# Batch 0's context quantised by column blocks with attention in between, later context turned by DMA, flips of context and weight scales moved to later tiles

## The chip, the core and the metric

One core of one Trainium2 chip. The engines of the core run their own programs, which meet at semaphores: PE (TensorE, matmuls), DVE (VectorE), ACT (ScalarE), POOL (GpSimd) and SP (SyncE, which here issues all loads, stores and DMA transposes). PEld is PE's weight load, which the profile lists apart from the matmul. The metric is the device time of one execution in microseconds (us).

## The reference

x is 4 batches of 512 tokens of width 512, ctx has the same shape. Two residual steps:

```python
x = x + _L0_xattn_ref(_layernorm(x), ctx_2048)        # xq @ wq^T, both quantised
x = x + _L0_ffn_ref(_layernorm(x), ...)

xq = quant_dequant_act_1x128(x)            # fp8 with one scale per token and 128 columns
wq = quant_dequant_weight_128x128(weight)  # fp8 with one scale per 128x128 block
return jnp.einsum('emk,enk->emn', xq, wq)

probs = jax.nn.softmax(xt @ w_router); topk_p, topk_idx = jax.lax.top_k(probs, 4)
basis = jax.nn.silu(xt @ w_gate) * (xt @ w_up)         # 8 bases of 256 columns
mixed = jnp.einsum('tek,tki->tei', mix[topk_idx], basis)
out = sum_e coeff_e * (mixed_e @ w_down)
shared = silu(xt @ shared_w_gate) * (xt @ shared_w_up) @ shared_w_down
return out + shared
```

The first step takes the batch's whole context (512 rows) as the weight: every tile of a batch needs all of it, quantised and turned so that columns lie on partitions.

## The kernel before

The 2048 tokens go in 16 tiles of 128; tiles 4b to 4b+3 belong to batch b. For each tile t the kernel does: layernorm of x; quantising it by blocks of 128 columns (DVE `quantise_x`: maxima, scale, mask; POOL `round_x`: an add and a subtract with a mask that rounds to the fp8 grid); turning x (PE `turn_x` in tiles 0 to 2, a DMA transpose from SP later); four attention matmuls `attend(t, kc)`, one for each block of 128 columns, into two PSUM tiles that take turns (even, odd); DVE `attention(t, kc)` scales each and adds it to x; layernorm to z (DVE `stats2`, ACT `norm2`, DVE z_lo); turning z as two fp16 halves (PE in tiles 0 and 1, SP's `turn_z` later); router logits (`route`), top four (DVE `largest`, `pick`), coefficients; five pairs of gate and up matmuls, p = -1 (the shared expert) and 0 to 3, whose results ACT (`silus`), DVE (`combine`) and POOL join; and the down projection `down(s)` of the tile before.

The matmuls of the gate, up and down weights run as three fp16 products (hi·hi, hi·lo, lo·hi). Tile 0 has no halves yet: `pair32` uses the fp32 weights as they were loaded, while ACT (`split_w`) and DVE (`lo_w`) make the halves chunk by chunk in tiles 0 and 1. There are twelve weight chunks in six groups (0,3), (3,5), (5,7), (7,9), (9,11), (11,12); the last chunk, DOWN, holds the down weights. A group's scale takes: ACT `sum_w` of each chunk, PE `flip_w` (the sums onto a few lanes), DVE `lane_w` (their maximum, a power of two, a small diagonal), PE `spread_w` (back to all 128 partitions), DVE `scales_w`. The context's scales go the same way, with DVE `max_ctx` in place of the sums: `flip_ctx(b)`, `lane_ctx`, `spread_ctx(b)`, `scales_ctx`.

The context of a batch is four chunks of 128 rows, c = 4b to 4b+3. Each is scaled (`scale_ctx`), masked on DVE (`mask_ctx`, two passes), rounded (`round_ctx`, two passes) into one of two `ctx_q` buffers, turned on PE (`turn_ctx`, four 128x128 transposes into the PSUM tile `turned[0]`) and copied by ACT (`keep_ctx`) to `ctx_qT`. For batch 0, DVE scales chunks 0 and 1 and rounds 2 and 3, ACT scales 2 and 3, POOL rounds 0 and 1; all four chunks are turned before the first attention matmul. For batch 1, ACT scales in tile 1. For batches 2 and 3, POOL scales. The turns of a later batch lie in two tiles of the batch before it; `ctx_turns(t)` gives them as `early` and `late`: all four of batch 1's in tile 2, batch 2's in tiles 5 and 6, batch 3's in tiles 9 and 10.

All of this is one function, `build`, which writes each engine's program out by hand, in order. PE's begins at the profile's line 1124; flips, spreads, turns and attention matmuls that belong to other work are put between two column steps of a pair by a dictionary: `pair32(0, {4: lambda: spread_w(2)})` puts the spread ahead of step 4 of the eight (four of gate, four of up). Of a tile t from 1 on, pair -1 and pair 0 carry the attention of tile t + 1, pair 2 its route; down(t - 1) stands behind pair 0 (down(0) at the end of tile 1). DVE's order begins at line 1556, ACT's at 765; SP's issues of a tile stand in the loop that begins at line 491. On every engine what is queued behind a waiting instruction waits too. PE's transposes share the two PSUM tiles `turned`, and the lists `uses0` and `uses1` say in which order, so that each user waits for the one before it.

The lines of before that the rows name:

| line | what |
|---|---|
| L899, L905 | PE `flip_ctx`, `spread_ctx` |
| L912, L920 | PE `flip_w`, `spread_w` |
| L929, L937, L969 | PE `turn_ctx`, `turn_x`, `turn_z32` (tile 0's z in fp32) |
| L954, L985, L1032 | PE `attend`, `pair32`, `pair` |
| L1014 | PE `route` |
| L1207, L1215 | DVE `max_ctx`, the lane's maximum in `lane_ctx` |
| L1233, L1239, L1242 | DVE `scale_ctx`, the two passes of `mask` |
| L1272, L1288 | DVE `stats`, first pass of `quantise_x` |
| L1317 | DVE `attention` |
| L1508, L1523, L1532 | DVE `lane_w`, `scales_w`, `lo_w` (gate_up, router and down halves) |
| L560, L567 | POOL `round_x`, add and subtract |
| L646, L655, L706 | ACT `sum_w`, `scale_ctx`, `norm2` of tile 0 |
| L460 | SP `turn_z`, low half |

Of the kernel before, what the change touches and what calls it, by code (L numbers as in the profile page):

```python
# [29 lines left out]
P = 128  # L30
# [43 lines left out]
def build(nc, x, ctx, w_router, w_gate, w_up, w_down, amplitudes, expert_scale,  # L74
# [35 lines left out]
    with ExitStack() as stack:  # L110
# [135 lines left out]
        ctx_scaled_dve, ctx_scaled_act, ctx_scaled_pool = sem("ctx_scaled_dve"), sem("ctx_scaled_act"), sem("ctx_scaled_pool")  # L246
# [3 lines left out]
        xT_in = sem("xT_in")  # L250
        zT_in = [sem("zT_hi_in"), sem("zT_lo_in")]
# [48 lines left out]
        def uses0():  # L300
# [3 lines left out]
            for t in range(1, TILES):  # L304
                front = t + 1 < TILES
                early, late = ctx_turns(t)
                if t % NB == 2 and t > 2:
                    early, late = late[:1], late[1:]
                out += [("coef", t)] + [("ctx", c) for c in early]
                out += [("ctx", c) for c in late] + [("weight", t + 1)] * front  # L310
            return out

        def uses1():
# [75 lines left out]
        def _(sp):  # L389
            def load_ctx(b, k):  # L390
                c = b * NB + k
                if b > 0:
                    wait_ctx_rounded(sp, c - NB)
# [7 lines left out]
            def load_chunk(n):  # L401
# [65 lines left out]

            def store(s):
# [22 lines left out]
            for t in range(TILES):  # L491
# [27 lines left out]
        def _(pool):  # L519
# [10 lines left out]
            def scale_ctx(c):  # L530
# [1184 lines left out]
```

## Time and profile before

| | |
|---|---|
| time, median of 3 runs (lowest to highest) | 588.35 us (586.7 to 589.03) |
| the profiled execution's own time | 587.09 us |
| its span in the trace, granted TensorE clock | 585.3 us, 0.994 |
| PE busy | 539.1 us, 92% of the span |
| DVE, ACT, POOL busy | 393.6 (67%), 242.8 (41%), 200.5 (34%) |
| chain of work that ended last | PE 73%, DVE 9%, issue 3%, ACT 2%, POOL 1% |
| DMA | 36.98 MB on queue q1, 23.4% of 16 engines |

The trace is of one execution, so its durations add up to its own 587.09, of which 585.3 is the span of the trace; the median stands 1.26 above it. PE is busy for 92% of the span as a mean, but the stages differ: a start without expert matmuls, tile 0 in fp32, tile 1 in which halves are still being made, and fourteen tiles after that. The rows that follow give the busy time for each stage. In brackets behind an instruction of a timeline stands the idle time of its engine just before it, with what released it. A clock of 1.00 in a row is TensorE's full clock.

### The profile page before, as it was taken

To read this page: it belongs to the slowest core of one execution; us is meant where nothing else is said; L and a number is where in the kernel's file an instruction comes from. 1 tells how busy PE (TensorE), PEld (TensorE's weight loads), DVE (VectorE), ACT (ScalarE), POOL (GpSimd) and SP (SyncE) were. 2 spreads that over 40 slices of the span, in tenths; PEclk is the share of its full clock that TensorE was granted. 3 is DMA by queue.
4 is the path that set the end of the run, shared out by engine and by line. 5 is a ranking of instruction groups with operands and counts; after the bars stand their busy time and mean duration, and the time that the engine had idled before them with its cause. 6 is when DMAs were issued, how large, how long until landed. Compare 5 with 4: busy or idle time off the path is not lost.

```text
span 585.3 us, 7951 instructions
## 1 busy us (share of the span) xinstructions
PE 539.1 (92%) x2624; PEld 257.8 (44%) x2624; DVE 393.6 (67%) x1123; ACT 242.8 (41%) x357; POOL 200.5 (34%) x236
## 2 busy tenths in 40 slices
PE   0359979789999999999999999999999999999997
PEld 0124434334544444454444444444444444444445
DVE  6977888788766577858574777768474757563322
ACT  4687885552524232342434242343433333423310
POOL 2431052443713126544413135634414131411110
PEclk9999999989999999999999999999999999999999
DMA  8724521011212413102113212111132111111110
GB/s 282 274 90 143 179 92 28 18 29 45 55 37 47 116 36 91 37 27 55 36 29 98 65 38 54 37 47 45 28 63 29 41 50 29 45 28 36 29 36 19
DMA packets 61657, 37.49 MB, mean 64 GB/s; under 512 B 48688, under 2 KB 49456, under 8 KB 61616
## 3 DMA queue, kind: packets, MB, share of 16 engines
q1 hardware_dynamic: 61616, 36.98, 23.4%
q8 instruction: 21, 0.34, 0.2%
q14 instruction: 20, 0.16, 0.1%
HBM read 21.24 MB, written 4.19 MB: 43 GB/s over the span
## 4 chain that ended last, share of the span: by engine, by line
PE 73%; DVE 9%; issue 3%; ACT 2%; POOL 1%; DVEq 0%
PE up L1032 29%; PE gate L1032 29%; PE even L1062 9%; PE odd L1014 2%; DVE x L1317 1%; DVE part L1409 1%; PE even L954 1%; PE odd L954 1%; DVE before L1356 1%; DVE gate_up L1532 1%; DVE down_lo L1532 1%; DVE ctx_m L1239 0%; PE up L1089 0%; PE gate L1089 0%; PE odd L1074 0%
## 5 line engine op out<-in xcount | busy, mean ns | idle before, releaser
L1032 PE MATMUL gate<-gate_up,zT_hi 128*128 128x512 f16 x592 | 177.0, 381 | 0.1
L1032 PE MATMUL up<-gate_up,zT_hi 128*128 128x512 f16 x592 | 177.1, 381 | 0.0
L731 ACT ACTIVATE silu<-gate,w_back 128x512 f32<-128x512 f32 x74 | 50.8, 687 | 170.4 <-PE gate L1032 169.5
L1032 PE MATMUL gate<-gate_up,zT_lo 128*128 128x512 f16 x296 | 112.9, 381 | 0.0
L1032 PE MATMUL up<-gate_up,zT_lo 128*128 128x512 f16 x296 | 112.7, 381 | 0.0
L1409 DVE SCALAR_TENSOR_TENSOR part<-up,coef,silu 128x256 f32<-128x256 f32 x126 | 55.0, 478 | 49.0 <-PE up L1032 40.6
L1032 PEld LDWEIGHTS gate<-gate_up,zT_hi 128*128 128x128 f16 x592 | 57.9, 100 | 65.2 <-issue 1.4
L589 POOL TENSOR_TENSOR hid<-hid,part 128x256 f32<-128x256 f32 x47 | 34.6, 736 | 148.2 <-DVE part L1409 148.2
L1032 PEld LDWEIGHTS up<-gate_up,zT_hi 128*128 128x128 f16 x592 | 57.0, 98 | 62.3 <-issue 1.1
L573 POOL TENSOR_TENSOR gain<-var,minus_half 128x1 f32<-128x1 f32 x16 | 11.3, 703 | 131.8 <-DVE neg_mean L1331 131.8
L1032 PEld LDWEIGHTS up<-gate_up,zT_lo 128*128 128x128 f16 x296 | 29.1, 98 | 35.3 <-issue 0.8
L1032 PEld LDWEIGHTS gate<-gate_up,zT_lo 128*128 128x128 f16 x296 | 29.0, 98 | 35.3 <-issue 0.6
L1317 DVE SCALAR_TENSOR_TENSOR x<-odd,both_scale,x 128x128 f32<-128x128 f32 x128 | 35.9, 342 | 11.1 <-PE odd L954 11.1
L695 ACT ACTIVATE y<-x,shift,gain 128x512 f32<-128x512 f32 x16 | 13.0, 812 | 57.1 <-POOL shift L575 57.1
L591 POOL TENSOR_TENSOR hid<-hid,part 128x256 f32<-128x256 f32 x47 | 34.3, 729 | 3.7
L560 POOL TENSOR_TENSOR x_v<-x_v,x_m 128x512 f32<-128x512 f32 x16 | 24.4, 1522 | 18.0 <-DVE x_m L1242 18.0
L1345 DVE TENSOR_SCALAR logit<-odd,w_back 128x128 f32<-128x128 f32 x15 | 5.2, 349 | 34.7 <-PE odd L1014 34.7
L544 POOL TENSOR_TENSOR ctx_in<-ctx_in,ctx_m 128x512 f32<-128x512 f32 x14 | 18.7, 1337 | 18.9 <-DVE ctx_m L1242 18.9
L1062 PE MATMUL even<-down_hi,hT_hi 128*128 128x512 f16 x90 | 22.4, 386 | 1.5 <-DVE x L1317 1.5
L586 POOL TENSOR_TENSOR hid<-part 128x256 f32<-128x256 f32 x16 | 12.0, 751 | 31.9 <-DVE part L1409 31.9
L1317 DVE SCALAR_TENSOR_TENSOR x<-even,both_scale,x_in 128x128 f32<-128x128 f32 x64 | 18.0, 344 | 7.1 <-PE even L954 7.1
L668 ACT COPY ctx_qT<-turn 128x512 bf16<-128x512 bf16 x16 | 9.3, 584 | 30.2 <-PE turn L929 30.2
(211 smaller groups left out, 840.5 us busy)
## 6 DMA issues: line engine op xcount, KB each, us to landing
ctx_in<-in_ctx SPq DMA_DIRECT2D x16, 256.0 KB, 4.0
x_in<-in_x SPq DMA_DIRECT2D x16, 256.0 KB, 2.9
out<-y_out SPq DMA_DIRECT2D x15, 256.0 KB, 2.2
stage<-in_L_ffn_w_gate SPq DMA_DIRECT2D x2, 1024.0 KB, 8.0
stage<-in_L_ffn_w_up SPq DMA_DIRECT2D x2, 1024.0 KB, 5.1
stage<-in_L_ffn_shared_w_gate SPq DMA_DIRECT2D x1, 1024.0 KB, 8.7
stage<-in_L_ffn_shared_w_up SPq DMA_DIRECT2D x1, 1024.0 KB, 9.8
ctx_qT<-in_L_ffn_w_up SPq DMA_DIRECT2D x1, 1024.0 KB, 12.9
```

The costliest lines, as they stand in the source:

```text
L544: ch.did(nc.gpsimd.tensor_tensor(ctx_in[:, k], ctx_in[:, k], ctx_m[:, k % 2], ALU.add))
L560: ch.did(nc.gpsimd.tensor_tensor(x_v[:], x_v[:], x_m[:], ALU.add))
L586: nc.gpsimd.tensor_tensor(mixed, one, two, ALU.add).then_inc(mix_acc, 1)
L589: nc.gpsimd.tensor_tensor(mixed, mixed, one, ALU.add).then_inc(mix_acc, 1)
L591: nc.gpsimd.tensor_tensor(mixed, mixed, two, ALU.add).then_inc(mix_acc, 1)
L695: nc.scalar.activation(y2[:], x2[:, t % 3, :], ACT.Identity, bias=shift2[:], scale=gain2[:]).then_inc(y2_done, 1)
L731: nc.scalar.activation(silu[:, k % 2, :], gate_ps[k % 2][:], ACT.Silu, scale=w_back[:, n:n + 1] if t else 1.0 / LN_GAIN).then_inc(silu_don ...
L954: nc.tensor.matmul(ps[:], x_qT[:, kc, :], ctx_qT[:, t // NB, kc, :], start=True, stop=True).then_inc(att_full, 1)
L1032: mm = nc.tensor.matmul(ps[:], zT[a][:, t % 2, kc, :], wgu[:, n - 1 + i, w, kc, :], start=(m == 0), stop=(m == 3 * KC - 1))
L1062: mm = nc.tensor.matmul(even_ps[:], hT[a][:, hc, :], wd[w][:, hc, :], start=(n == 0), stop=(n == 3 * HC - 1))
L1317: ch.did(nc.vector.scalar_tensor_tensor(x2[:, t % 3, cols], ps[:, cols], both_scale[:, nb, kc:kc + 1], prev, ALU.mult, ALU.add))
L1409: ins = nc.vector.scalar_tensor_tensor(part[:, p % 2, cols], up_ps[k % 2][:, cols], coef[:, t % 2, KPC * p + i:KPC * p + i + 1], silu[:, k ...
```

## The change

What is computed, and the loads and stores, stay. Six things move.

1. **Batch 0's context by columns.** The `c` of batch 0's `scale_ctx`, `mask_ctx`, `round_ctx` and `turn_ctx` now means a block of 128 columns of all four row chunks (`ctx_cols`), which is what one `attend(0, kc)` needs. Blocks 0 and 2 are scaled on ACT, 1 and 3 on POOL; DVE masks and rounds all four and does attention of block kc - 2 after block kc. PE turns block by block with `attend` in between. The views are strided: 4 pieces of 128 columns a partition.
2. **Tile 0's x.** DVE takes its maxima (`measure_x`) ahead of the context's lane, and rounds it itself (`round_x`), where POOL did.
3. **Later contexts.** The twelve `turn_ctx` on PE and their `keep_ctx` on ACT go; SP issues twelve `dma_start_transpose`, early ones ahead of `turn_z(t + 1)`, late ones behind it. All of them are rounded on POOL as before.
4. **Scales of batch 1's context.** The maxima are the last thing on DVE in tile 1 (before: in the middle of it), flip and spread and lane come in tile 2, and ACT scales all four chunks in a row in tile 2 (before: two and two in tile 1).
5. **Scales of the weight groups 4 and 5.** Flips and spreads move from the last pair of tile 0 to the first two pairs of tile 1, `lane_w` and `scales_w` from tile 0 to the head of tile 1, `sum_w(DOWN)` on ACT into tile 1. In tile 0 the flips and spreads of groups 0 to 3 move by some steps.
6. **Small moves.** `norm2(0)` and `keep_z32` on ACT ahead of the first weight splits, `turn_x(2)` to the head of tile 1 from two steps later, `lo_w(DOWN)` on DVE ahead of `largest(2)`, `mask_ctx` of early chunks behind `combine(t, 0)`.

```diff
@@ uses1(): order of the second turning tile
-            out = lane("ctx", 0) + lane("w", 0) + [("x", 0)] + lane("w", 1) + [("x", 1)]
-            out += lane("w", 2) + lane("w", 3) + [("z", 1)] + lane("w", 4) + lane("w", 5)
+            out = lane("ctx", 0) + [("x", 0)] + lane("w", 0) + [("flip_w", 1), ("x", 1), ("spread_w", 1)]
+            out += lane("w", 2) + lane("w", 3) + [("z", 1)] 
...
+        def ctx_cols(kc):
+            return ctx_in[:, :, kc * P:(kc + 1) * P]
...
@@ SP
+            def turn_ctx(c):
+                b, k = c // NB, c % NB
+                if c == NB:
+                    wait_ready(sp, DOWN)
+                sp.wait_ge(ctx_round_pool, CTX_ROUNDS * (c - NB + 1))
+                sp.dma_start_transpose(ctx_qT[:, b, :, k * P:(k + 1) * P], ctx_q[:, c % 2, :]).then_inc(ctxT_in[c % 2], 16)
...
+                for c in early:
+                    turn_ctx(c)
                 if 2 <= t + 1 < TILES:
                     turn_z(t + 1)
+                for c in late:
+                    turn_ctx(c)
                 if 3 <= t + 2 < TILES:
                     turn_x(t + 2)
...
@@ POOL scale_ctx
-                nc.gpsimd.tensor_tensor(c4(ctx_in[:, k]), c4(ctx_in[:, k]),
-                                        ctx_mul[:, k].unsqueeze(2).to_broadcast([P, KC, P]), ALU.mult
+                rows, by = (ctx_cols(c), ctx_mul[:, :, c]) if c < NB else (by_block(ctx_in[:, k]), ctx_mul[:, k])
+                nc.gpsimd.tensor_tensor(rows, rows, by.unsqueeze(2).to_broadcast([P, KC, P]), ALU.mult
...
@@ ACT
+                if t == 2:
+                    for c in range(NB, 2 * NB):
+                        scale_ctx(c)
...
@@ PE attend(t, kc)
-                    pe.wait_ge(kept0, turn_of(HI, "ctx", t // NB * NB + NB - 1) + 1)
+                    if t >= NB:
+                        for i in range(2):
+                            pe.wait_ge(ctxT_in[i], 8 * NB * (t // NB))
...
@@ PE tile 0
-            pair32(3, {0: lambda: route(1), 1: lambda: flip_w(4), 4: lambda: spread_w(4), 5: lambda: flip_w(5)})
-            spread_w(5)
...
+            pair32(-1, {4: lambda: flip_w(1), 6: lambda: turn_x(1)})
+            pair32(0, {2: lambda: [spread_w(1), attend(1, 0)], 4: lambda: attend(1, 1), 7: lambda: flip_w(2),
+                       6: lambda: attend(1, 2)})
+            pair32(1, {0: lambda: [turn_weight(0), attend(1, 3)], 2: lambda: spread_w(2), 3: lambda: coefs(0),
+                       7: lambda: flip_w(3)})
+            pair32(2, {2: lambda: spread_w(3), 6: lambda: [turn_z(1, HI), turn_z(1, LO)]})
+            pair32(3, {0: lambda: route(1)})
...
@@ PE tile t
+                    shared[0] = lambda: turn_x(2)
+                    shared[5] = lambda: flip_w(4)
+                if t == 2:
+                    shared[3] = lambda: flip_ctx(1)
...
+                    zero[0] = lambda: [spread_w(4), coefs(1)]
+                    zero[4] = lambda: flip_w(5)
+                    zero[7] = lambda: spread_w(5)
+                if t == 2:
+                    zero[1] = lambda: spread_ctx(1)
...
@@ DVE start
+            x_chain = measure_x(0)
             scales_ctx(lane_ctx(0), 0)
-            scale_ctx(0)
-            scale_ctx(1)
-            mask_ctx(0)
-            mask_ctx(1)
-            quantise_x(0)
-            lane_chain = lane_w(0)
...
+            shrink_x(x_chain, 0)
+            round_x(0)
+            for kc in range(KC):
+                mask_ctx(kc)
+                round_ctx(kc)
+                if kc >= 2:
+                    attention(0, kc - 2)
+            attention(0, 2)
             stats(1)
+            attention(0, 3)
+            stats2(0)
```

How the built programs stand, one instruction or a run of like ones a row (line, operation, out<-in, shape, count). First PE from the flip of batch 0's context scales to the first expert matmul, which is L985 before and L983 after; `turn` is the PSUM tile of transposes, `even` and `odd` those of attention. Before:

```order
L899 MATMUL turn<-ident,ctx_max 16x128
L905 MATMUL turn<-lane_diag,ones 128x16
L929 MATMUL turn<-identb,ctx_q 128x128 x4
L912 MATMUL turn<-ident,w_max 3x128
L920 MATMUL turn<-lane_diag,ones 128x3
L929 MATMUL turn<-identb,ctx_q 128x128 x8
L937 MATMUL turn<-identb,x_q 128x128 x4
L929 MATMUL turn<-identb,ctx_q 128x128 x4
L954 MATMUL even<-ctx_qT,x_qT 128x512
L954 MATMUL odd<-ctx_qT,x_qT 128x512
```

After:

```order
L931 MATMUL turn<-identb,x_q 128x128 x4
L923 MATMUL turn<-identb,ctx_q 128x128 x8
L952 MATMUL even<-ctx_qT,x_qT 128x512
L923 MATMUL turn<-identb,ctx_q 128x128 x4
L952 MATMUL odd<-ctx_qT,x_qT 128x512
L906 MATMUL turn<-ident,w_max 3x128
L923 MATMUL turn<-identb,ctx_q 128x128 x4
L952 MATMUL even<-ctx_qT,x_qT 128x512
L952 MATMUL odd<-ctx_qT,x_qT 128x512
L959 MATMUL turn<-ident,y 128x128 x4
L914 MATMUL turn<-lane_diag,ones 128x3
```

x is turned ahead of all context, the attention matmuls stand between the turns, and the first flip and spread of weight scales (L912, L920 before, L906, L914 after) go behind the second attention matmul and behind z's turn.

Then ACT in tile 2, from the shared silu of tile 2 (`hs_hi` is the half that `down(1)` needs, `hid_abs` the shared expert's sums, `y`, `z_hi` the norm of tile 3). Before:

```order
L744 ACTIVATE hs_hi<-hid,hid_scale 128x768
L731 ACTIVATE silu<-gate,w_back 128x512
L738 ACTIVATE hid_abs,shared_sum<-hid 128x512
L695 ACTIVATE y<-x,shift,gain 128x512
L701 ACTIVATE z_hi<-x,shift,gain 128x512
L677 ACTIVATE y<-x_in,neg_mean 128x512
```

After:

```order
L761 ACTIVATE hs_hi<-hid,hid_scale 128x768
L748 ACTIVATE silu<-gate,w_back 128x512
L675 ACTIVATE ctx_in<-ctx_in,ctx_mul 128x128 x16
L755 ACTIVATE hid_abs,shared_sum<-hid 128x512
L712 ACTIVATE y<-x,shift,gain 128x512
L718 ACTIVATE z_hi<-x,shift,gain 128x512
```

The scaling of all four chunks of batch 1 now stands between the silu of pair 0 and the sums and norm behind it; before, it was done in tile 1.

Last SP in tile 2, from the stores of tiles 0 and 1 to the turn of tile 4's x. Before:

```order
L470 DMA out<-y_out 128x512 x2
L458 DMA_TRANSPOSE zT_hi<-z_hi 128x4x128
L460 DMA_TRANSPOSE zT_lo<-z_lo 128x4x128
L466 DMA_TRANSPOSE x_qT<-x_q 128x4x128
L399 DMA x_in<-in_x 128x512
```

After:

```order
L483 DMA out<-y_out 128x512 x2
L479 DMA_TRANSPOSE ctx_qT<-ctx_q 128x4x128 x2
L462 DMA_TRANSPOSE zT_hi<-z_hi 128x4x128
L464 DMA_TRANSPOSE zT_lo<-z_lo 128x4x128
L479 DMA_TRANSPOSE ctx_qT<-ctx_q 128x4x128 x2
L470 DMA_TRANSPOSE x_qT<-x_q 128x4x128
```

Two turns of context now stand ahead of the turn of tile 3's z, and two between it and the turn of x.

## Rows read from the trace of the kernel before

**Rows 1.** Stretches of the span: length, busy us per engine (instructions), PE clock, DMA.

```profile
40.20:86.07 45.87, 41.70 (x127) 18.50 (x127) 36.46 (x98) 38.99 (x42) 13.00 (x12) 1.00 0.40 132
86.07:127.83 41.76, 36.44 (x165) 15.96 (x165) 34.77 (x81) 21.49 (x34) 13.44 (x13) 0.92 0.12 26
127.83:161.72 33.89, 32.62 (x174) 15.77 (x173) 28.13 (x70) 14.57 (x26) 19.29 (x20) 1.00 0.19 47
161.72:193.28 31.56, 31.56 (x158) 14.94 (x157) 19.30 (x62) 11.16 (x17) 8.79 (x12) 1.00 0.25 61
```

**Rows 2.** PE timeline, start: start us, us, engine, line, what, [idle before].

```profile
38.33 2.08 PE L969 MATMUL odd<-y_out 128*128 128x128 f32 x8 [1.24 <-ACT y_out L706]
...
40.20 1.92 PE L985 MATMUL gate<-stage,y_out 128*128 128x512 f32 x2
```

**Rows 3.** PE timeline, end of tile 0 and of tile 1.

```profile
77.02 0.27 PE L912 MATMUL turn<-ident,w_max 128*2 128x128 f32 x1 [1.49 <-ACT gate_up L646]
...
82.98 0.27 PE L912 MATMUL turn<-ident,w_max 128*1 128x128 f32 x1 [1.75 <-DVE w_back L1523]
...
113.72 0.28 PE L899 MATMUL turn<-ident,ctx_max 128*16 128x128 f32 x1 [2.44 <-DVE ctx_max L1207]
...
114.71 1.06 PE L1032 MATMUL gate<-gate_up,zT_hi 128*128 128x512 f16 x2
...
119.98 0.39 PE L905 MATMUL turn<-lane_diag,ones 16*128 16x16 f32 x2 [1.71 <-DVE lane_diag L1217]
```

**Rows 4.** PE timeline, a context turn in tile 2, next matmul.

```profile
147.86 0.39 PE L929 MATMUL turn<-identb,ctx_q 128*128 128x128 bf16 x4
148.08 0.59 PE L1032 MATMUL up<-gate_up,zT_hi 128*128 128x512 f16 x2
```

**Rows 5.** DVE timeline, start and tiles 0 and 1.

```profile
7.31 0.69 DVE L1207 TENSOR_REDUCE ctx_max<-ctx_in 128x4 f32<-128x512 f32 x1 [0.19 <-DMA ctx_in<-in_ctx]
...
8.55 0.28 DVE L1215 TENSOR_REDUCE lane_top<-turn 16x1 f32<-16x128 f32 x1 [0.56 <-PE turn L899]
...
10.29 1.29 DVE L1233 TENSOR_TENSOR ctx_in<-ctx_in,ctx_mul 128x512 f32<-128x512 f32 x2
...
23.58 0.41 DVE L1239 TENSOR_SCALAR ctx_m<-ctx_in 128x512 uint32<-128x512 uint32 x1
...
25.83 0.69 DVE L1272 BATCH_NORM_STATS2 stat<-x_in 128x6 f32<-128x512 f32 x1
...
28.20 1.12 DVE L1317 SCALAR_TENSOR_TENSOR x<-even,both_scale,x_in 128x128 f32<-128x128 f32 x4
...
33.64 0.74 DVE L1532 SCALAR_TENSOR_TENSOR router_lo<-y_out,w_scale,router_hi 128x512 f16<-128x512 f32 x1
...
34.30 0.68 DVE L1288 TENSOR_REDUCE x_max<-y 128x4 f32<-128x512 f32 x1
...
36.96 2.35 DVE L1532 SCALAR_TENSOR_TENSOR gate_up<-stage,w_scale,gate_up 128x2048 f16<-128x2048 f32 x1
...
63.87 0.27 DVE L1508 TENSOR_REDUCE lane_top<-turn 2x1 f32<-2x128 f32 x1
...
64.69 2.33 DVE L1532 SCALAR_TENSOR_TENSOR gate_up<-ctx_qT,w_scale,gate_up 128x2048 f16<-128x2048 f32 x1
...
119.85 3.40 DVE L1532 SCALAR_TENSOR_TENSOR down_lo<-ctx_qT,w_scale,down_hi 128x3072 f16<-128x3072 f32 x1
```

**Rows 6.** POOL timeline, rounding of tile 1's x.

```profile
37.12 3.32 POOL L560 TENSOR_TENSOR x_v<-x_v,x_m 128x512 f32<-128x512 f32 x1 [2.06 <-DVE x_m L1242]
40.52 1.27 POOL L567 TENSOR_TENSOR x_q<-x_v,x_m 128x512 bf16<-128x512 f32 x1
```

**Rows 7.** ACT timeline, scaling of two context chunks in tile 1.

```profile
123.66 2.45 ACT L655 ACTIVATE ctx_in<-ctx_in,ctx_mul 128x128 f32<-128x128 f32 x8 [4.24 <-DVE ctx_mul L1226]
```

**Rows 8.** Timeline of SP and of PE, z of tile 2 to router.

```profile
105.64 1.27 SPq L460 DMA_TRANSPOSE zT_lo<-z_lo  x1
...
108.22 0.22 PE L1014 MATMUL odd<-router_hi,zT_hi 128*128 128x128 f16 x1 [0.81 <-issue]
```

More of the change, by code:

```diff
@@ L250, in build @@
         xT_in = sem("xT_in")
+        ctxT_in = [sem(f"ctxT_in{i}") for i in range(2)]
         zT_in = [sem("zT_hi_in"), sem("zT_lo_in")]
@@ L305, in uses0 @@
                 front = t + 1 < TILES
[L306 to L310, printed above, removed]
+                out += [("coef", t)] + [("weight", t + 1)] * front
             return out
@@ L612, in _ @@
                 mix_parts(t - 1, 3)
-                for c in early:
-                    round_ctx(c)
                 if t % NB == 1 and 0 < b < B - 1:
@@ L625, in _ @@
                     rstd_of(t + 2)
+                for c in early:
+                    round_ctx(c)
                 for c in late[:1]:
@@ L649, in scale_ctx @@
             def scale_ctx(c):
-                k = c % NB
                 act.wait_ge(ctx_lane, CTX_LANE * (c // NB + 1))
-                for kc in range(KC):
+                for i in range(KC):
+                    k, kc = (i, c) if c < NB else (c % NB, i)
                     part_k = ctx_in[:, k, kc * P:(kc + 1) * P]
@@ L828, in _ @@
                     norm1(t + 2)
-                if t % NB == 2 and t > 2:
-                    for c in late[:1]:
-                        keep_ctx(c)
                 silus(t, 1)
@@ L1126, in _ @@
             spread_ctx(0)
+            turn_x(0)
             turn_ctx(0)
+            turn_ctx(1)
+            attend(0, 0)
+            turn_ctx(2)
+            attend(0, 1)
             flip_w(0)
+            turn_ctx(3)
+            attend(0, 2)
+            attend(0, 3)
+            turn_z32()
             spread_w(0)
-            turn_ctx(1)
-            turn_ctx(2)
-            turn_x(0)
-            turn_ctx(3)
-            for kc in range(KC):
-                attend(0, kc)
-            turn_z32()
-            route32()
-            pair32(-1, {1: lambda: flip_w(1), 4: lambda: spread_w(1), 6: lambda: [turn_x(1), attend(1, 0)]})
-            pair32(0, {2: lambda: [attend(1, 1), flip_w(2)], 4: lambda: spread_w(2), 5: lambda: attend(1, 2),
-                       7: lambda: [turn_weight(0), attend(1, 3)]})
-            pair32(1, {2: lambda: coefs(0), 5: lambda: flip_w(3), 7: lambda: spread_w(3)})
-            pair32(2, {5: lambda: [turn_z(1, HI), turn_z(1, LO)]})
-            pair32(3, {0: lambda: route(1), 1: lambda: flip_w(4), 4: lambda: spread_w(4), 5: lambda: flip_w(5)})
-            spread_w(5)
+            route32()
+            pair32(-1, {4: lambda: flip_w(1), 6: lambda: turn_x(1)})
[5 more added lines that the diff above has]
+            pair32(3, {0: lambda: route(1)})
             for t in range(1, TILES):
@@ L1645, in _ @@
                     stats(t + 2)
+                if t == 2:
+                    scales_ctx(ctx_chain, 1)
                 coefficients(t)
                 combine(t, 0)
+                for c in early:
+                    mask_ctx(c)
                 if t > 1:
@@ L1656, in _ @@
                     combine(1, 1)
-                    for c in range(NB, 2 * NB):
-                        max_ctx(c)
                 if b == 0:
@@ L1683, in _ @@
                     pick(top_chain, u)
+                if t == 1:
+                    for c in range(NB, 2 * NB):
+                        max_ctx(c)
             part_half(0)
```

196 lines of the change are left out of this document (80 added, 116 removed).

## The prediction, made before the changed kernel was run

> **What bounds the kernel now.** I read the stretches first. Tile 3 takes 31.56 us and PE is busy for all of it; tile 2 takes 33.89 with 1.27 of PE idle; tile 1 takes 41.76; tile 0's fp32 pairs take 45.87 [rows 1]. So from tile 3 on PE sets the pace, and only work taken off PE counts there. Then the timeline of PE: the first expert matmul starts at 40.20 [rows 2]. Before tile 2 stand waits of 1.49, 1.75, 2.44 and 1.71 us, all for a flip or spread of scales, and after 113.72 the clock falls: two matmuls that take 0.59 at 2.4 GHz take 1.06 [rows 3]. Tile 1 is 10 us longer than tile 3 by these waits and that clock. What comes before those waits runs on DVE, which I therefore follow. Times of the changed kernel below are my own, added up from row durations.
>
> **Steady tiles.** Twelve turns of later context leave PE. One holds it 148.08 − 147.86 = 0.22 us [rows 4]: 2.6 in all, 0.9 of it in tile 2 and 1.74 in tiles 5, 6, 9 and 10. ACT's copies behind them go too; ACT waits for PE anyway, so nothing for that. The turns by DMA are not in the trace; nearest is z's, 2.6 from issue to the matmul that needs it [rows 8]. In tiles 5 to 10 they start a tile ahead, so PE work covers that or twice that: **−1.74**.
>
> **Start.** The last context maximum starts at 7.31 and takes 0.65. DVE then measures x (1.0 of the 36.96 − 34.30 = 2.66 that a quantise takes), and does the context lane, 10.29 − 8.55 = 1.74 [rows 5]: 10.7. X's scaling and masks take the other 1.65, its rounding 1.35; then each column block's mask and round 25.83 − 23.58 = 2.25 [rows 5]. Two scalings now run on POOL beside x's masks; I charge one POOL pass of 1.3 (1.27, [rows 6]; bounds 0 and 2.6). So the x turn is ready at 15.0, blocks at 17.2, 19.4, 21.7, and after one attention step (1.04, [rows 5]) the fourth at 25.0. Three attention steps, tile 1's statistics (1.2) and 0.3 of waits end at 29.6, tile 0's statistics at 30.7, against 33.64: 2.9 earlier. From there to the first expert matmul it was 40.20 − 33.64 = 6.56 [rows 2, 5]; 1.0 goes, since the copy of z no longer stands behind a weight split on ACT. First expert matmul at 36.25: **−3.95**. If the column views cost the masks their speed (0.41 becomes the 0.69 of other passes, four times) it is −2.8; if POOL hinders nothing, −5.2.
>
> On POOL x's add takes 3.32 where a 2.35 us weight pass of DVE starts with it, against 1.27 for the pass behind it [rows 5, 6]. The Trainium skill (SBUF — State Buffer, Who interferes with whom) calls the ports shared by DVE and GpSimd an exclusive lock, and says a DVE instruction with two SBUF inputs contends with GpSimd's reads too. By it x's multiply and adds could also wait for the two scalings; this term would then be −2.7. These rows agree on the lock, and do not show it for such adds.
>
> **Tile 0.** The flips that PE waited for (1.49, 1.75) move to tile 1, with their spreads (0.85 of matmuls, 0.6 of gaps around them); old waits of 0.9 for x_qT and attention go too: −4.75. New waits come, because DVE now stands at the head of its queue for PE twice: the first weight spread follows turn_z32 (DVE idle 31.6 to 34.2), the second follows turn_x(1) (44.2 to 47.7). So tile 1's x is quantised at 39.0 instead of 37.0; its POOL rounding under the lock takes 4.7 (37.12 to 41.79, [rows 6]), to 43.75, where PE stands from 42.8: +0.95. The third attention step waits for DVE at 52.55, PE is there at 51.5: +1.1. The coefficients wait for ACT's weights (+0.55), the flip of group 3 for ACT's sum (+1.0), turn_z(1) for z_lo (+1.0), turn_x(2), now at the head of tile 1, for POOL (+1.05): +5.65 less 0.9 that the cover of the cold start hides. Sum **0.0**; tile 1 starts at 36.25 + 45.87 = 82.1. Each of the six waits is a difference of two of my times, so ±2.
>
> **Tile 1.** The waits 2.44 and 1.71 go, and the half-speed stretch: PE was busy 36.44 where tile 3 needs 31.56 [rows 1], and the flips and the x turn explain 1.4 of that, so the clock cost about 3.5, 1.7 to a wait. In their place the lanes of weight groups 4 and 5 stand on DVE ahead of tile 2's statistics, 64.69 − 63.87 = 0.82 each [rows 5] and 0.3 for their scales. PE's waits become: spread 0.4, attention 1.05, router(2) 1.55 (z_lo at 103.6, then 2.6, [rows 8]; PE is there at 104.95), ACT's silu 0.3. The last is down: the split of its weights on ACT ends at 111.6, DVE's quantise at 112.3, its pass of 3.40 [rows 5] at 115.7; PE is there at 114.0: +1.7. So 31.56 + 5.0 + 0.9 for the moved flips = 37.5 against 41.76: **−4.26**, tile 2 at 119.6.
>
> **Tile 2.** The 0.9 of turns and the 1.27 wait go. The context flip comes, behind four maxima on DVE: +1.1, and 0.3 of matmuls. Then ACT: the scaling of four chunks stands ahead of abs_shared and norm2(3) and waits for ctx_lane, which DVE writes behind two statistics at 135.3. ACT idles from 130.4; the sixteen activations take 4.9 (eight take 2.45, [rows 7]), to 140.2; z_hi(3) is at 142.4 and not 136.7. On SP two context turns stand ahead of turn_z(3); the second waits for POOL, whose four passes take 5.3 from 137.8 (1.27 each and gaps, [rows 6]), to 143.1, and each issue holds SP 1.2 (1.27, [rows 8]). z_lo's turn is issued at 145.55, router(3) starts at 148.15, PE is there at 145.5: +2.65. Bounds: 0 if SP and ACT are free in time, 5 if the turns queue. DVE's combine (149.9) and the silus behind are in time. So 35.8 against 33.89: **+1.9**.
>
> A turn costs PE 0.22 [rows 4]. The Trainium skill (VectorE: DVE Perf Modes, Rules for kernel authors) speaks against this part: transpose 128×128 on TensorE if a PSUM destination will do, and by crossbar DMA otherwise. By it the 2.6 would be kept on PE and 2.65 at router(3) saved, some 0.1 in all. The rows bear it out at router(3) alone; elsewhere PE is the scarce engine.
>
> **The sum.** −3.95 + 0.0 − 4.26 + 1.9 − 1.74 = −8.05. The profiled execution took 587.09, so 579.0; the median shown is 1.26 above it: 580.3.
>
> **Rivals.** (a) The new waits of tiles 0 to 2 mostly stay away, because one earlier POOL pass sets the others right. Half of 5.65 + 5.0 + 2.65 saved is 6: about 574.5. For it: outside the flips PE had 0.9 of waits in tile 0. Against: the six have different causes.
> (b) DVE binds harder: 1.5 more in the start (views and lock) is carried along DVE to tile 2's router, which then starts at 108.2 as now. From there down's weights come at 117.4, tile 2 at 121.3: −6.5 + 1.9 − 1.74 = −6.3, with another 1.5 for the clock about 583.5. For it: the lanes stand ahead of the statistics. Against: DVE also sheds two scalings and four maxima there.
> (c) What is won is given back in tile 2: router(3) waits 5 instead of 2.65, and the clock falls after it and after down, at 1.7 each as in tile 1: 580.3 + 2.35 + 3.4 = 586, no change.
> (d) Slower: PE stays at 1.2 GHz through fp32 pairs. Before, two matmul instructions took 1.92 at the start of the first pair [rows 2], and later ones 0.86. If the new waits at turn_x(1) and attend(1,2) keep the clock down through two or three pairs, at 6.84 more each, the gain of 8 turns to +6 to +12: 594 to 600. It decides from 11 us, under two pairs. Against: the waits of 1.49 and 1.75 left the matmuls behind them at full speed.
> (e) That the change does not do what it says: the built order has the twelve turns on SP and none on PE, so only their price can differ, which is (c).
>
> **Chances.** Forecast 0.49, (a) 0.12, (b) 0.22, (c) 0.12, (d) 0.05. The range takes in the forecast with its bounds, (b) and most of (a): 575.0 to 585.5. Half a per cent (2.9 us) is about what a measurement of this kernel can tell from no change. Faster by more: forecast, (a), (b), 0.83; same (c), 0.12; slower (d), 0.05.
>
> **What would show it.** Right: the first expert matmul near 36; tile 1 near 82; no PE wait for ctx_max in tile 1 nor for w_max at the end of tile 0; a wait of down for down_lo of 1 to 2 us; in tile 2 ACT idle ahead of sixteen scalings and PE idle at router(3) of about 2.6; tile 3 still at 31.56, tiles 5 and 6 shorter by 0.44. Wrong: PE waits of over 3 us in tile 0, or a granted clock below 1 over more than 10 us.

## The result, and the profile after

The changed kernel takes 582.86 us (median of 4 runs, 581.85 to 583.85) where the kernel before takes 588.29: a ratio of 0.9914, 95% interval 0.9893 to 0.9934. It is faster, by 0.9% where 1.4% was forecast, and lies in the range that was given (575.0 to 585.5). The profiled execution took 582.28. One execution of a later run (e5) took 959.96 at a mean granted clock of 0.572 and is left out there.

The page of the changed kernel, its span and the busy time of the engines:

```profile
span 580.5 us, 7864 instructions
PE 534.5 (92%) x2576; PEld 254.6 (44%) x2576; DVE 396.8 (68%) x1127; ACT 234.4 (40%) x344; POOL 198.0 (34%) x232
```

The same stretches as in [rows 1] (tile 0's fp32 pairs, tiles 1, 2 and 3), cut at the first gate matmul of each:

```profile
37.09:82.60 45.51, 40.53 (x125) 17.94 (x125) 38.33 (x94) 38.56 (x43) 13.48 (x9) 1.00 0.34 115
82.60:121.42 38.82, 33.53 (x166) 15.14 (x164) 33.92 (x82) 23.40 (x26) 17.84 (x15) 1.00 0.16 40
121.42:159.71 38.29, 34.05 (x161) 15.91 (x160) 34.63 (x82) 15.62 (x33) 20.78 (x22) 0.96 0.24 55
159.71:191.27 31.56, 31.56 (x158) 14.92 (x157) 19.30 (x62) 11.16 (x17) 9.25 (x13) 1.00 0.31 78
```

Set against [rows 1, 2], in us of the two profiled executions:

| stretch | before | after | change | forecast |
|---|---|---|---|---|
| start, to the first expert matmul | 40.20 | 37.09 | -3.11 | -3.95 |
| tile 0 | 45.87 | 45.51 | -0.36 | 0.0 |
| tile 1 | 41.76 | 38.82 | -2.94 | -4.26 |
| tile 2 | 33.89 | 38.29 | +4.40 | +1.9 |
| tiles 3 to 15 and end | 423.58 | 420.79 | -2.79 | -1.74 |
| sum | 585.3 | 580.5 | -4.80 | -8.05 |

Up to tile 2 the changed kernel is 6.4 ahead; tile 2 gives 4.4 of it back. The larger waits of PE from 30 us on (line, released by, us in total, times, longest); the one ahead of them, of 5.6, is for tile 0's z and still belongs to the start:

```profile
PE odd L1012 <- issue: 4.7, 2, 3.2
PE turn L931 <- POOL x_q L588: 2.1, 2, 1.5
PE even L1060 <- DVE down_lo L1533: 2.0, 1, 2.0
PE even L952 <- DVE x L1318: 1.9, 2, 1.0
PE turn L995 <- DVE z_lo L1340: 1.2, 1, 1.2
PE turn L893 <- DVE ctx_max L1198: 1.1, 1, 1.1
PE turn L914 <- DVE lane_diag L1516: 1.0, 2, 0.7
...
PE even L1060 <- DVE x L1318: 0.5, 2, 0.2
```

L1012 is the router, L931 turn_x, L1060 down, L952 attend, L995 turn_z, L893 the flip of the context's scales, L914 the spread of weight scales. The four waits of [rows 3] are gone from their places; these stand instead. The largest is router(3), in tile 2. PE's timeline there:

```profile
150.96 0.27 PE L1012 MATMUL odd<-router_hi,zT_hi 128*128 128x128 f16 x1 [3.15 <-issue]
...
152.19 1.06 PE L1030 MATMUL up<-gate_up,zT_hi 128*128 128x512 f16 x2
```

The stretches behind it, with the granted clock as the third number from the end:

```profile
151.00:152.20 1.20, 1.20 (x13) 1.20 (x14) 1.17 (x3) 0.00 (x0) 1.12 (x2) 0.50 0.55 109
152.20:153.40 1.20, 1.20 (x5) 0.44 (x4) 1.17 (x2) 0.00 (x0) 0.70 (x1) 0.50 0.00 0
```

Behind the wait PE runs at 1.2 GHz: the router's twelve matmuls take 1.23 (150.96 to 152.19) where router(2) took 0.67, the two columns after it 2.34 (to 154.53) where they took 1.30: 1.6 lost. What held z of tile 3, in the timelines of ACT and SP:

```profile
137.61 4.79 ACT L675 ACTIVATE ctx_in<-ctx_in,ctx_mul 128x128 f32<-128x128 f32 x16 [4.83 <-DVE ctx_mul L1217]
...
144.04 0.34 SPq L483 DMA_DIRECT2D out<-y_out  x1
144.49 2.54 SPq L479 DMA_TRANSPOSE ctx_qT<-ctx_q  x2
147.12 1.21 SPq L462 DMA_TRANSPOSE zT_hi<-z_hi  x1
148.38 1.26 SPq L464 DMA_TRANSPOSE zT_lo<-z_lo  x1
```

ACT idles 4.83 for the context's scales, scales for 4.79, and only then makes z, whose high half is done at 144.42. SP, which had waited 11.7 for DVE's y_out of tile 1, stores it at 144.04, turns two context chunks with no wait between them, 1.2 to 1.3 each, and then z.

### The profile page after: what moved, and what is told of

Same layout as the page of the kernel before. It is cut to its first block, busy times and chain, and to the rows that moved or that the text cites. A ratio compares the mean times of both kernels' runs of the same rounds, so it can differ in the third digit from the quotient of the medians.

```text
span 580.5 us, 7864 instructions
## 1 busy us (share of the span) xinstructions
PE 534.5 (92%) x2576; PEld 254.6 (44%) x2576; DVE 396.8 (68%) x1127; ACT 234.4 (40%) x344; POOL 198.0 (34%) x232
## 4 chain that ended last, share of the span: by engine, by line
PE 73%; DVE 8%; issue 3%; POOL 2%; DMA 1%; ACT 1%; SPq 0%; DVEq 0%; POOLq 0%; ACTq 0%
PE up L1030 29%; PE gate L1030 29%; PE even L1060 9%; PE odd L1012 2%; DVE x L1318 2%; PE odd L952 1%; PE even L952 1%; DMA zT_hi<-z_hi 1%; DVE gate_up L1533 1%; DVE part L1410 1%; DVE down_lo L1533 1%; POOL gain L594 0%; POOL ctx_in L563 0%; PE up L1087 0%; PE gate L1087 0%
## 5 line engine op out<-in xcount | busy, mean ns | idle before, releaser
L581 POOL TENSOR_TENSOR x_v<-x_v,x_m 128x512 f32<-128x512 f32 x15 | 26.2, 1745 | 20.3 <-DVE x_m L1225 20.3
L1060 PE MATMUL even<-down_hi,hT_hi 128*128 128x512 f16 x90 | 21.9, 379 | 2.5 <-DVE down_lo L1533 2.0
L1060 PE MATMUL even<-down_lo,hT_hi 128*128 128x512 f16 x90 | 21.9, 379 | 0.0
L1060 PE MATMUL even<-down_hi,hT_lo 128*128 128x512 f16 x90 | 21.9, 379 | 0.0
```

Of the source, the lines that this page charges most:

```text
L581: ch.did(nc.gpsimd.tensor_tensor(x_v[:], x_v[:], x_m[:], ALU.add))
L1060: mm = nc.tensor.matmul(even_ps[:], hT[a][:, hc, :], wd[w][:, hc, :], start=(n == 0), stop=(n == 3 * HC - 1))
```

## Experiments

All are the changed kernel with the edit shown; times are medians, beside 588.6, 587.95 and 587.81 for the kernel before in the three groups of runs (e1 to e4, e5 to e8, e9 to e11). Where a few tenths matter I compare the traces by the time at which PE turns a tile's top-four weights (`turn_weight` in pair -1, the same instruction in each kernel): in the changed kernel tile 1's is at 85.19, tile 2's at 125.38, tile 5's at 225.96, tile 13's at 479.82. Line numbers differ by a few between kernels.

### What holds router(3): e1, e2, e3

e1, on SP:

```diff
+                if t == 2:
+                    early, late = [], early + late
                 for c in early:
                     turn_ctx(c)
```

> The changed kernel with one edit: on SP in tile 2 all four turns of context stand behind the turn of tile 3's z. In the changed kernel router(3) waits 3.15 us and PE then runs at half clock, which costs some 1.7 more. Theory SP (the queue is the last link): z_hi's turn is issued when z_hi is done (144.4), z_lo's at 146.3, the router starts at 148.9 where PE is there at 147.65, so the wait falls to 1.2; with the clock kept 579.1, with it lost all the same 580.8. Theory ACT (sixteen scalings ahead of the norm are the only cause): the wait stays at 3.2 and the time at 582.9.

Measured 580.19 (ratio 0.987, 0.9856 to 0.9885). The turns of context now stand last, and the wait is a third of what it was:

```profile
146.58 1.19 SPq L464 DMA_TRANSPOSE zT_lo<-z_lo  x1
147.87 8.12 SPq L479 DMA_TRANSPOSE ctx_qT<-ctx_q  x4
...
149.09 0.22 PE L1014 MATMUL odd<-router_hi,zT_hi 128*128 128x128 f16 x1 [1.01 <-issue]
```

e2, on ACT and DVE:

```diff
-                if t == 2:
-                    for c in range(NB, 2 * NB):
-                        scale_ctx(c)
...
                     norm2(t + 1)
+                if t == 2:
+                    for c in range(NB, 2 * NB):
+                        scale_ctx(c)
...
-                for c in early:
-                    mask_ctx(c)
...
                     z_lo(u)
+                for c in early:
+                    mask_ctx(c)
```

> The changed kernel with the other edit: on ACT in tile 2 the sums and the norm of tile 3 stand ahead of the sixteen scalings, and DVE's z_lo(3) ahead of the first two context masks; SP's order as in the changed kernel. Theory ACT: z_hi is done at 138.5 where it was 144.4, z_lo at 140, the router is in time: wait 0, clock kept, tile 2 shorter by 5: 577.9. Theory SP: the two context turns ahead of z's turn still wait for POOL to round the second chunk, which now starts later; z's turns go out at 147.5 and 148.8, the router at 151.3: wait 3.3 or more, 582.9 or up to 1 longer.

Measured 583.41 (0.9917, 0.9904 to 0.9929), no gain, and the wait is longer. z_hi was done at 138.7; its turn went out at 148.04, behind the context's two, for which SP waited 3.9 and 1.4 until POOL had rounded them:

```profile
SPq L478 <- POOL ctx_q L569: 3.9, 1, 3.9
...
144.16 3.78 SPq L479 DMA_TRANSPOSE ctx_qT<-ctx_q  x2
148.04 1.21 SPq L462 DMA_TRANSPOSE zT_hi<-z_hi  x1
...
151.87 0.25 PE L1012 MATMUL odd<-router_hi,zT_hi 128*128 128x128 f16 x1 [3.89 <-issue]
```

e3 has both edits.

> Both edits of the two runs before. Theory series (either of the two alone holds the router, so both must go): z_hi done at 138.5, its turn issued at once, router(3) at 142.6 or whenever PE is there: wait 0, no half clock, tile 2 at 31.56 + 1.09 (context flip) + 0.5 = 33.2 where the changed kernel has 38.29: 577.8. Rival (the context turns come too late behind z's turn, so that POOL and DVE queue up behind them and the combine of tile 2 stalls PE): part of the 5 comes back as waits of PE for DVE in pairs 2 and 3: 579 to 582.

Measured 579.87 (0.9851, 0.9837 to 0.9865): router(3) waits for nothing, but only 0.3 is gained over e1, which is not clear of noise (the two profiled spans are equal, 578.2). The rival came true: DVE waits for POOL ahead of its last two context masks, quantising tile 4's x stands behind these, and the combine of pair 1, for which pair 3 waits, behind that:

```profile
144.49 1.41 DVE L1224 TENSOR_SCALAR ctx_m<-ctx_in 128x512 uint32<-128x512 uint32 x1 [1.24 <-POOL ctx_q L571]
...
154.75 0.61 PE L1032 MATMUL up<-gate_up,zT_hi 128*128 128x512 f16 x2 [1.94 <-DVE part L1412]
```

So SP's order is the last link, ACT's the one before it, DVE's the next.

### What the clock costs: e11

```diff
             def route(t):
+                if t == 3:
+                    pe.wait_ge(att_step, ATT_STEPS * (t + 1))
+                    for i in range(14):
+                        nc.tensor.matmul(odd_ps[:], zT[HI][:, (t - 1) % 2, 0, :], wgu[:, 0, HI, 0, :],
+                                         start=True, stop=True)
```

> The changed kernel with fourteen matmuls of no use (into the PSUM tile that router(3) then overwrites) ahead of router(3), 14 x 0.216 = 3.0 us, so that PE works while it waits there for z of tile 3. The router itself can start no earlier. Theory clock (the idle time makes the clock fall, which costs 1.7 after it): the granted clock stays at 1.00, router and the next four columns take 0.67 and 2.6 as elsewhere, tile 2 is 1.7 shorter: 581.2. Rival (the clock falls for another reason, such as what other engines do): 0.5 from 151 on as before, 582.9 or more.

Measured 580.69 (0.9883, 0.9866 to 0.99). Work of no use saves 2.2 us by the medians; the router starts as late in its tile as without it, and the clock stays. PE's timeline:

```profile
147.39 3.19 PE L1003 MATMUL odd<-gate_up,zT_hi 128*128 128x512 f16 x14
```

The stretch behind it:

```profile
151.00:153.40 2.40, 2.40 (x20) 1.34 (x18) 2.33 (x4) 0.00 (x0) 1.69 (x1) 1.00 0.25 50
```

From tile 2's turn of weights to tile 5's it is 98.96 where the changed kernel needs 100.58: 1.62, the price of one fall. One trace would not show the cause, since e9's lost no clock after a like wait (last section); but all four executions of e11 (580.39 to 581.09, mean clock 0.997 to 1.000) are shorter than all four of the changed kernel (581.85 to 583.85, 0.994 to 0.997).

### POOL beside DVE: e5, e6

e5: POOL's `scale_ctx(1)` and `scale_ctx(3)` go, ACT does blocks 0 to 3 in a row:

```diff
             norm1(0)
             scale_ctx(0)
+            scale_ctx(1)
             scale_ctx(2)
-            sum_w(0)
+            scale_ctx(3)
             keep_x(0)
+            sum_w(0)
```

> The changed kernel, but batch 0's context is scaled on ACT alone (four blocks in a row, the copy of x and the first weight sum behind them); POOL does nothing in the start. In the changed kernel DVE's scaling of x takes 1.54 and its first mask 1.16 while POOL scales, 0.69 and 0.43 elsewhere. Theory POOL: both return to 0.69 and 0.43, x's turn and all after it comes 1.58 earlier, the first expert matmul at 35.5 where it was 37.09, and tile 0, whose waits hang on DVE, carries it: 581.3. Rival ACT (its scalings, or the loads of weights, slow DVE): the two passes stay long, first expert matmul at 37.1 or later, 582.9.

Measured 580.99 (0.9874, 0.9856 to 0.9892). DVE and POOL in the changed kernel's timeline, then DVE in that of e5:

```profile
11.08 1.54 DVE L1296 TENSOR_TENSOR x_v<-y,x_mul 128x512 f32<-128x512 f32 x1
12.66 1.16 DVE L1222 TENSOR_SCALAR x_m<-x_v 128x512 uint32<-128x512 uint32 x1
...
11.04 2.50 POOL L555 TENSOR_TENSOR ctx_in<-ctx_in,ctx_mul 128x512 f32<-128x512 f32 x2 [4.60 <-DVE ctx_mul L1217]
```

```profile
11.23 0.69 DVE L1296 TENSOR_TENSOR x_v<-y,x_mul 128x512 f32<-128x512 f32 x1
11.95 0.43 DVE L1222 TENSOR_SCALAR x_m<-x_v 128x512 uint32<-128x512 uint32 x1
```

The first expert matmul is at 35.66 (37.09), and tile 1's and tile 5's turns of weights are 1.43 and 1.35 earlier: what the start gains stays.

e6, on DVE in tile 1:

```diff
                     scales_w(lane_chain, 5)
-                    lo_w(9)
...
                 if t == 1:
+                    lo_w(9)
                     lo_w(10)
```

> The changed kernel, but in tile 1 DVE makes the low half of weight chunk 9 behind z_lo(2) and not ahead of the statistics of tile 3's x. In the changed kernel POOL's power for the norm of tile 2's z starts with that pass and takes 2.72 us where others take 0.55; router(2) waits 1.55. Theory lock: the power takes 0.6, z_hi is done 2 us earlier, z_lo at 102.6, the router waits for nothing and all of tile 1 is 1.5 earlier: 581.4. Rival (the power is slow by itself, or DVE's row of work sets z_lo): router(2) waits 1 to 1.6 as now: 582.9.

Measured 579.98 (0.9869, 0.9851 to 0.9887). POOL's power of one column, first in the changed kernel:

```profile
99.47 2.72 POOL L594 TENSOR_TENSOR gain<-var,minus_half 128x1 f32<-128x1 f32 x1 [9.40 <-DVE neg_mean L1332]
```

And in e6:

```profile
99.37 0.55 POOL L594 TENSOR_TENSOR gain<-var,minus_half 128x1 f32<-128x1 f32 x1 [9.40 <-DVE neg_mean L1332]
```

The durations in both runs agree with the exclusive lock that the Trainium skill describes (SBUF — State Buffer, Who interferes with whom): it is the later of the two instructions that takes longer, x's multiply, which starts 0.04 behind POOL's scaling in the changed kernel, and the power, which starts 0.03 behind DVE's pass. For x's multiply the prediction had left that open.

Router(2)'s wait of 1.55 is gone, and tile 2's turn of weights comes 2.25 earlier. How much of this is the lock's is not shown. The pass that moved also stood ahead of z_lo(2) in DVE's own order, and in the changed kernel DVE, which idles no more than 0.2 at a time from the pass on, reaches z_lo just when ACT has z_hi done (104.01):

```profile
99.44 2.34 DVE L1533 SCALAR_TENSOR_TENSOR gate_up<-stage,w_scale,gate_up 128x2048 f16<-128x2048 f32 x1
...
104.10 0.69 DVE L1340 TENSOR_TENSOR z_lo<-y,z_hi 128x512 f16<-128x512 f32 x1
```

In e6 both are 2.3 earlier, z_hi at 101.74 and z_lo at 101.83. So the expectation's rival, DVE's row of work, is taken away by the same edit and is not ruled out.

### Do waits that are taken away stay away: e4, e9, e7, e10

e4, on DVE in tile 1:

```diff
-                    quantise_x(t + 2)
+                if t == 1:
+                    x_chain = measure_x(3)
+                    lo_w(DOWN)
+                    shrink_x(x_chain, 3)
+                elif ahead:
+                    quantise_x(t + 2)
...
-                if t == 1:
-                    lo_w(DOWN)
```

> The changed kernel, but in tile 1 DVE makes the low half of the down weights right behind the maxima of tile 3's x and ahead of the rest of its quantising (1.8 us). down(0) waits 2.03 us for it in the changed kernel. It can start when ACT's split ends, 112.66, and end at 116.1, PE is there at 115.3: wait 0.7. Theory local: the time falls by 1.3 to 1.4, to 581.5. Theory DVE (DVE's row of work up to the context maxima sets the next wait): the maxima of batch 1's context end at 124.9 as before or 0.4 later while PE is there 1.4 earlier, so the wait at the context flip grows from 1.09 to about 2.7 and the time stays at 582.9, within 0.5.

Measured 583.72 (0.993, 0.9911 to 0.9948): no gain. down(0) waits 1.26 less, the next wait is 1.84 longer:

```profile
116.33 1.47 PE L1060 MATMUL even<-down_hi,hT_hi 128*128 128x512 f16 x6 [0.77 <-DVE down_lo L1533]
...
125.27 0.28 PE L893 MATMUL turn<-ident,ctx_max 128*16 128x128 f32 x1 [2.93 <-DVE ctx_max L1198]
```

e9, part 5 of the change undone (DVE's and ACT's lines move with it):

```diff
-            pair32(3, {0: lambda: route(1)})
+            pair32(3, {0: lambda: route(1), 1: lambda: flip_w(4), 4: lambda: spread_w(4), 5: lambda: flip_w(5)})
+            spread_w(5)
```

> The changed kernel with one part undone: flips, spreads and lanes of the weight groups 4 and 5, and ACT's sum of the down weights, stand at the end of tile 0 again. PE then waits there: some 2.4 us for ACT's sum of chunk 10 (77.7, PE is at 75.3), 1.3 for the last lane on DVE, and 0.8 for the matmuls: tile 1 starts 4.9 later, at 87.5. Theory local (each wait of PE counts): tile 1 gives back only the 1.0 of its own flips and spreads: 3.9 more, 586.8. Theory DVE (its row of work sets router(2) in both orders): DVE reaches tile 2's statistics at the same time, since it does the same work by then, and PE's waits in tile 1 (0.66, 0.90, 1.55) go for those in tile 0: 0 to 0.5 more, 583 to 583.4.

Measured 584.91 (0.9951, 0.9936 to 0.9965), between the two. PE waits at the end of tile 0 as expected:

```profile
77.16 0.27 PE L905 MATMUL turn<-ident,w_max 128*2 128x128 f32 x1 [2.08 <-ACT gate_up L666]
...
83.61 0.27 PE L905 MATMUL turn<-ident,w_max 128*1 128x128 f32 x1 [1.75 <-DVE w_back L1519]
```

Tile 1's turn of weights is 4.79 later (4.9 was expected), tile 2's only 0.96: four fifths come back, so DVE's row decides most of it. The median is 2.05 above the changed kernel's; the profiled execution, 581.59, is one in which the clock never fell. The other 1.1 is probably falls of the clock, since the mean clock is 0.991 to 0.994 in six of seven runs; no trace of mine shows them.

e7 joins e1, e2, e4, e5 and e6, and moves two things more:

```diff
-                    shared[3] = lambda: flip_ctx(1)
+                    shared[5] = lambda: flip_ctx(1)
...
+                if t == 2:
+                    combine(t, 1)
                 if b == 0:
                     for c in late:
                         mask_ctx(c)
```

> All edits so far together, with two more that the earlier runs call for: the combine of pair 1 in tile 2 stands ahead of the last two context masks (pair 3 waited 1.94 for it), and the flip of batch 1's context scales two steps later in tile 2. Sum of what each would give alone: start 1.5, router(2) 1.5, down(0) 1.3, context flip 1.1, tile 2 3.0 (measured) and 1.9: 10.3, so 572.6. Theory waits (each is a wait of its own): 572 to 574. Rival DVE (its row of work runs without gaps from tile 0 to tile 2, so that a wait taken away returns at the next thing that DVE does): half of it, 577 to 578.

Measured 576.2 (0.9807, 0.9793 to 0.9822), 6.7 less than the changed kernel and two thirds of the sum, of which 1.3 was down(0)'s, where e4 alone had gained nothing. In place of down(0)'s wait stand two others:

```profile
112.03 1.47 PE L1062 MATMUL even<-down_hi,hT_hi 128*128 128x512 f16 x6 [0.62 <-DVE down_lo L1535]
...
120.97 0.28 PE L895 MATMUL turn<-ident,ctx_max 128*16 128x128 f32 x1 [1.52 <-DVE ctx_max L1200]
...
122.72 0.38 PE L954 MATMUL even<-ctx_qT,x_qT 128*128 128x512 bf16 x1 [0.83 <-issue]
```

e10 is e7 without e4's edit.

> All edits together as in the run before, but the low half of the down weights stands behind the quantising of tile 3's x again. In the run with all edits down(0) waited 0.62, but the context flip 1.52 and the attention of tile 3 0.83, since x of tile 3 came later. Theory DVE (one row of work, so taking a wait away at down(0) only moves it): down(0) waits 1.9, the flip 0.2, attention 0: 0.8 less, 575.4. Theory local: 1.3 more, 577.5.

Measured **575.18** (0.9786, 0.9772 to 0.98). That is 1.0 below e7 by the medians, part of it clock: two of e7's five executions have a mean clock of 0.997, none of e10's is below 0.999. By the traces e10 needs 0.56 less from tile 0's turn of weights to tile 3's (100.21 and 100.77). So the theory of DVE's row is right and theory local is not: down(0) waits 1.89 again, the flip waits for nothing, and no time is lost by it.

The attention of tile 3 does still wait. Its matmul is missing from the trace, so that the idle time stands ahead of the next one, but its weight load is there. It waits for the PSUM tile `even`, which DVE reads for `y_out` until 122.57, and not for x of tile 3, which went out to be turned at 116.31 (2.4 us to landing by the median):

```profile
121.82 0.75 DVE L1450 SCALAR_TENSOR_TENSOR y_out<-even,out_scale,x 128x512 f32<-128x512 f32 x1
122.64 0.10 PEld L954 LDWEIGHTS even<-ctx_qT,x_qT 128*128 128x128 bf16 x1 [1.16 <-issue]
122.89 0.59 PE L1032 MATMUL up<-gate_up,zT_hi 128*128 128x512 f16 x2 [0.91 <-issue]
...
154.45 0.33 PE L1040 MATMUL turn<-ident,weight 128*128 128x128 f32 x1 [1.03 <-DVE weight L1369]
...
159.91 0.39 PE L954 MATMUL even<-ctx_qT,x_qT 128*128 128x512 bf16 x1 [0.67 <-DVE x L1320]
```

The last two lines are in tile 3, where the changed kernel and e3 have no wait; e7 has the same two (1.04 and 0.67). So where the combine was moved ahead, the 1.94 of e3 is gone and 1.7 of waits for DVE have come behind it.

Not every wait comes back. By tile 5's turn of weights e3 is 2.26 ahead of the changed kernel, e5 1.35 and e6 2.30, 5.91 together; e10, which has all three, is 6.94 ahead. So these three add up in full. The two pieces added in e7, for which 1.9 and 1.1 were expected, bring the other 1.0 at most.

This version beats both kernels, by 2.1% and 1.3%.

### The turns by DMA: e8

Turns and copies of batches 2 and 3 stand on PE and ACT again, at the steps of the kernel before:

```diff
+                if late and t % NB == 2:
+                    pair(t, 1, {7: lambda: turn_ctx(late[0])})
+                    second[4] = lambda: turn_ctx(late[1])
+                else:
+                    pair(t, 1)
+                    if late:
+                        second[4] = lambda: turn_ctx(late[0])
+                        third[3] = lambda: turn_ctx(late[1])
```

> The changed kernel with one part undone: the contexts of batches 2 and 3 are turned on PE and copied by ACT again, at the steps of the kernel before; batch 1 stays on DMA. Theory PE time alone (0.22 us a turn, eight turns): 1.8 more, 584.7. Theory PE and ACT (the copies also hold the silu that the combine waits for, so that the down projections of tiles 6 and 10 wait 0.75 where they wait 0.23): 2.8 more, 585.7. Rival (a turn hides in gaps of PE): 582.9.

Measured 584.48 (0.9935, 0.9921 to 0.9948). Between the turns of weights of tiles 5 and 13 lie 256.66 us, 253.86 in the changed kernel: 2.80. That is 1.8 of PE time and 1.0 of waits at down in tiles 6 and 10, which are back (PE's waits: total, times, longest):

```profile
PE even L1074 <- DVE x L1340: 1.5, 2, 0.7
```

The median says 1.6; it scatters by what the clock costs, the trace does not.

## Why the prediction was right, and where not

The path and the direction were right: old waits leave tiles 0 and 1, new ones come at the places named, and tile 2 gets longer. The trace gained 4.80 where 8.05 was forecast. Of the 3.25 that are missing, 2.5 lie in tile 2 (1.6 of them a fall of the clock), 1.3 in tile 1 and 0.8 in the start; tile 0 and the steady tiles came out better, by 0.4 and 1.05.

**Start.** Sequence and cover were right: tile 0's statistics end at 31.6, and from there to the first expert matmul it took 5.5 (5.56 was worked out); PE's wait there for ACT's copy of z, 1.24 in [rows 2], is 0.21 (L706 of before is this copy, `keep_z32`, and not `norm2`). POOL's scaling cost DVE 1.58 and not the 1.3 that was charged (e5); the other 0.5 lies ahead of it, mostly because the last context maximum ended at 8.37 where the sum had 7.96. The column views cost the masks nothing (0.42 and 0.43 a pass).

**Tile 0.** Of the six waits forecast, the ones at turn_x(1) (0.95 forecast), attend(1,2) (1.1), turn_z(1) (1.0) and turn_x(2) (1.05) came as 1.47, 1.02, 1.23 and 0.67; the coefficients and the flip of group 3 did not wait more than 0.22. The sum behind this term was wrong: 1.49, 1.75, 0.85, 0.6 and 0.9 add to 5.59 and not to 4.75, so that its own terms give −0.84. Measured is −0.36: PE was busy 1.17 less (41.70 to 40.53) and idle 0.81 more. That the 0.0 came this close is luck.

**Tile 1.** Waits at the places named: spread 0.66 (0.4), attention 0.90 (1.05), router(2) 1.55 (1.55), down 2.03 (1.7). The term was 1.3 too good: 0.4 in these waits, about 0.6 because each of four waits costs some 0.16 more than the idle time shows (at down the last column starts at 115.12, takes 0.22, and the next matmul starts at 117.53: 2.19 for a wait of 2.03), the rest in flips and spreads. That no clock was lost here was right for this execution. That router(2)'s wait agrees to the digit is luck: the forecast's own z_lo at 103.6, 2.6 and PE at 104.95 give 1.25. Both came 1.2 later (104.79 and 106.18), and z_lo's turn went out another 0.5 later, behind z_hi's.

**Tile 2.** This step failed. The wait was found, with its two causes in the right order (e1, e2), and sized at 2.65 against 3.15. What it does to the clock was left out of the forecast and put into rival (c) at 1.7; it is 1.6 (e11). With 0.5 at the wait, 0.3 around its two waits and 0.1 in flips that is the 2.5 that tile 2 took more than forecast.

**Steady tiles.** Mis-sized to the good side: the turns themselves give the 1.74; that nothing else goes with them was wrong: 1.0 of waits at down in tiles 6 and 10 does (e8). Whether ACT's copies, which can hold a silu and so the combine, or the turns' own 0.22 bring these is not settled; e8 moves both.

**Rivals.** The outcome lies between forecast and rival (c), and by its time nearest to (b) (583.5). (b)'s marks came too: router(2) at 107.89 (108.2 in (b)) and tile 2 at 121.42 (121.3; 119.6 in the forecast). Its cause came in part: the start lost 0.8 and not 1.5, the clock 1.6 at router(3). That DVE's row of work carries a wait from place to place, e4 and e9 show, and the combine in e7 and e10. (a) fell: the waits came (half of its three terms is 6.65 and not 6, which makes 573.7). (d) fell: the fp32 pairs ran at the full clock but for the first eight matmuls, which took 4.01 where eight took 3.49 from 74.61 on. (e) fell.

## What to carry to other kernels

A queue that issues transfers is an engine like the others: an issue put ahead of another costs that its own time, here twice 1.2 us, of which PE paid 2.1 and the clock on top, and in e2 the wait for its producer as well. Where one engine's row of work causes several waits, a wait that is taken away by putting other work of that row later tends to come back at the later place (e4, the combine in e7 and e10); what shortens the row (e5), or moves a pass to where the engine idles (e6, where DVE's 2.58 of idle time at 110.10 takes it in), stays. Put one-column work of POOL where DVE isn't in a long pass: the power took 2.72 beside one and 0.55 without.

## What was not expected of the hardware

The same wait does not always cost the clock. In the changed kernel's trace 3.15 us at router(3) were followed by 0.50; in e9's trace 3.13 us at the same place were not. With a wait of 3.1 to 3.9 us there, six traces show the fall (the changed kernel, e2, e4, e5, e6 and e8), and e9's alone does not:

```profile
151.80:154.50 2.70, 2.61 (x21) 1.57 (x22) 2.63 (x4) 0.00 (x0) 1.99 (x2) 1.00 0.24 49
```

A wait of 2.03 at down(0) left the clock alone in the changed kernel, while in e2's trace 2.04 brought it to 0.60:

```profile
117.28:121.50 4.22, 4.22 (x12) 1.58 (x13) 3.83 (x13) 2.47 (x4) 2.81 (x3) 0.60 0.15 30
```

The four runs of the changed kernel fall in two pairs by their mean clock, 0.997 (581.85, 582.28) and 0.994 (583.44, 583.85), some 1.6 apart, which is one fall; e10, with no wait above 1.9, lies within 0.7 us at 0.999 to 1.000. The Trainium skill (TensorE: Matmul & The Clock Gate, Part 1: The HAM clock gate) says that the chip's activity window runs freely, so that the point of change varies from run to run; these traces agree in that like waits end differently, and do not show the window itself.
